# Two decoder layers with gated cross attention and expert routing: roots, slots and weighted bias rows move from VectorE to GpSimd, and the turning of exponentials stands one quarter row further behind the scores

## The reference

```python
# 32 batches, 128 query rows, 120 context rows, width 128, 16 heads of 8, 8 experts, top 2
x = x + tanh(g_xattn[0]) * xattn0(layernorm(x), ctx, ctx, group_prob, mask)   # softmax * group_prob
x = x + tanh(g_ffn[0])   * ffn0(layernorm(x))        # top-2 of 8 experts with a capacity, gelu, 512 hidden
x = x + tanh(g_xattn[1]) * xattn1(layernorm(x), ctx, ctx, mask1)
x = x + tanh(g_ffn[1])   * ffn1(layernorm(x))        # all 8 experts, weighted by the top-2 scores

def layernorm(x, eps=1e-5):
    m, v = mean(x, -1), var(x, -1)
    return (x - m) / sqrt(v + eps)
# ffn0: probs = softmax(x @ Wg); the top two with gates; position of a token in its expert by a running
# count; tokens past the capacity are dropped; rows scattered to the experts, gathered back, times gate.
# ffn1: out = sum_e ((h_a * sigmoid(h_b)) @ Wo.T + bo) * comb[e];  h = x @ W1[e].T + b1[e]
```

## Time and profile before

| | |
|---|---|
| median of 3 runs | 1053.52 us (1051.51 to 1056.82) |
| profiled execution, device time | 1046.87 us |
| its span, first to last instruction | 1045.1 us |
| mean granted TensorE clock | 0.902 |
| busy: PE / DVE / ACT / POOL | 76% / 64% / 59% / 54% |

### The profile page before, as it was taken

One profiled execution on the slowest core, in us unless ns is written; L12 is line 12 of the kernel. 1 busy time (PEld: TensorE's weight loads), 2 busy tenths in 40 slices (PEclk: granted clock), 3 DMA queues, 4 the chain that ended last, 5 costly groups with the idle time before them and its releaser, 6 DMA issues.

```text
span 1045.1 us, 20666 instructions
## 1 busy us (share of the span) xinstructions
PE 796.5 (76%) x6552; PEld 627.2 (60%) x6552; DVE 668.9 (64%) x1992; ACT 611.4 (59%) x2578; POOL 559.8 (54%) x762
## 2 busy tenths in 40 slices
PE   2379888878852899990156778677877799999997
PEld 1256665656641799990035555555655577888885
DVE  1369989889863222210347778789888878666664
ACT  1369888778840444440146877687888645444442
POOL 7355566686556000002676875865421176777775
PEclk9679999999985899996558998999999899999998
DMA  7869734565334222225136365633530000000000
GB/s 179 207 175 272 163 94 112 110 157 131 89 86 164 62 72 71 72 59 161 45 81 146 99 146 98 151 96 59 124 72 12 21 21 21 21 21 21 11 11 21
DMA packets 80069, 97.56 MB, mean 93 GB/s; under 512 B 7952, under 2 KB 67285, under 8 KB 79000
## 3 DMA queue, kind: packets, MB, share of 16 engines
q1 hardware_dynamic: 75864, 87.99, 33.0%
q0 software_dynamic: 4096, 8.25, 3.3%
HBM read 59.18 MB, written 41.58 MB: 96 GB/s over the span
## 4 chain that ended last, share of the span: by engine, by line
PE 27%; issue 26%; POOL 18%; DVE 16%; ACT 10%; DMA 2%; POOLq 0%; SPq 0%; DVEq 0%; ACTq 0%
ACT exp L640 7%; PE psum L557 5%; PE psum L559 5%; PE psum L558 5%; POOL got_rows L1214 4%; DVE shift L815 4%; POOL scratch_xe L1207 3%; PE psum L407 3%; POOL full L1175 2%; PE psum L420 2%; PE psum L383 1%; DVE exp_T L825 1%; POOL ln_rstd L1143 1%; POOL parts L1185 1%; DVE ln_stats L785 1%
## 5 line engine op out<-in xcount | busy, mean ns | idle before, releaser
L640 ACT ACTIVATE exp<-psum,shift 128x120 f32<-128x120 f32 x1024 | 362.8, 400 | 140.4 <-DVE shift L815 139.6
L640 ACT ACTIVATION_READ_ACCUMULATOR exp<-psum,shift 128x1 f32 x1024 | 246.3, 244 | 0.0
L407 PE MATMUL psum<-ident,exp 128*120 128x128 f32 x1024 | 169.5, 291 | 79.5 <-ACT exp L640 47.5
L815 DVE TENSOR_REDUCE shift<-psum 128x4 f32<-128x480 f32 x256 | 165.5, 646 | 64.2 <-PE psum L398 63.6
L407 PEld LDWEIGHTS psum<-ident,exp 128*120 128x120 f32 x1024 | 118.6, 144 | 114.9 <-ACT exp L640 112.2
L1279 POOL TENSOR_TENSOR q_operand<-q_operand 128x512 f32<-128x512 f32 x96 | 126.1, 1313 | 61.8 <-DVE q_operand L1088 57.0
L1088 DVE SCALAR_TENSOR_TENSOR q_operand<-psum,comb,q_operand 128x256 f32<-128x256 f32 x256 | 111.5, 478 | 66.4 <-ACT q_operand L753 66.3
L753 ACT ACTIVATE q_operand<-psum 128x512 f32<-128x512 f32 x128 | 76.3, 599 | 112.9 <-PE psum L559 112.8
L395 PE MATMUL psum<-neg_rows,const_bf 128*128 128x480 bf16 x256 | 98.7, 385 | 35.8 <-issue 19.7
L557 PE MATMUL psum<-w_T_high,xn_T_high 128*128 128x512 f32 x256 | 106.9, 417 | 5.4 <-DVE w_T_low L1054 4.2
L559 PE MATMUL psum<-w_T_high,xn_T_low 128*128 128x512 f32 x256 | 101.3, 396 | 0.0
(11 more groups left out here) (135 smaller groups left out, 1649.9 us busy)
## 6 DMA issues: line engine op xcount, KB each, us to landing
q_operand<-scratch_q SPq DMA_DIRECT2D x32, 384.0 KB, 6.3
k_operand<-scratch_k SPq DMA_DIRECT2D x32, 360.0 KB, 9.3
scratch_q<-parts SPq DMA_DIRECT2D x16, 384.0 KB
scratch_k<-parts SPq DMA_DIRECT2D x16, 360.0 KB
scratch_q<-parts SPq DMA_DIRECT2D x16, 256.0 KB
scratch_xe<-in_zero_rows SPq DMA_DIRECT2D x8, 512.0 KB, 11.2
scratch_k<-parts SPq DMA_DIRECT2D x16, 240.0 KB
xe_rows<-scratch_xe SPq DMA_DIRECT2D x16, 192.0 KB, 2.7
```

The source lines that it names most:

```text
L407: ins = pe.transpose(ps[0:S2, T_BANKS[G % 2], u * S:(u + 1) * S], atts[l].expS[:, G % RING_E, u, :], ident[:, :])
L640: ins = act.activation(atts[l].expS[:, G % RING_E, u, :], ps[:, S_BANKS[G % 3], u * S2:(u + 1) * S2], ACT.Exp, bias=atts[l].shift[:, i % 2 ...
L815: dve.tensor_reduce(atts[l].shift[:, i % 2, 4 * r:4 * r + 4], ps[:, S_BANKS[G % 3], 0:4 * S2].rearrange("p (h k) -> p h k", h=4), AX_X, AL ...
```

## The change

- `rstd` leaves VectorE. Its Newton step is done in `powers` on GpSimd, as four dependent instructions on 128x4 values; the product with the mean is dropped, as normalising now subtracts the mean and multiplies by the root. Normalising of the far tables moves from offset 6 to 5.
- `slots` moves to GpSimd, as nine instructions (the integer slot is written by a copy of its own), in `POST` offset 24; sends wait for count 23 of `rt`.
- `add_bo` moves to GpSimd: one product over four batches into a new buffer `bo_part`, one addition. The sum of the weights stays on VectorE, at the end of `combination`.
- The lags of turning, inverse, inverse rows, sums and scaling each grow by one slot, and with them all `POST` steps. The ring of exponential buffers has four instead of three entries.
- ScalarE's `take_exps` of layer 1 stands before the exponentials of its slot instead of behind them.

```diff
@@ -49,7 +49,7 @@
 RING_O = 8
-RING_E = 3
+RING_E = 4
@@ -60,9 +60,9 @@
-LAG_TURN, LAG_INV, LAG_ROWS, LAG_SUM, LAG_O = 2, 5, 7, 8, 9
...
-ROUTE_STEPS = 25
+LAG_TURN, LAG_INV, LAG_ROWS, LAG_SUM, LAG_O = 3, 6, 8, 9, 10
...
+ROUTE_STEPS = 26
 WEIGH_STEPS = 17
@@ -89,10 +89,10 @@
 NEAR = dict(k_project=0, k_take=1, k_part0=1, k_left0=1, k_part1=2, k_left1=2, k_out=(1, 2, 3), k_fetch=12,
-            stat=0, power=1, rstd=2, norm=3, turn=4, turned=5, bias=8,
+            stat=0, power=1, norm=3, turn=4, turned=5, bias=8,
             q_project=5, q_take=6, q_part0=6, q_left0=6, q_part1=7, q_left1=7, q_out=(6, 7, 8), q_fetch=12)
 FAR = dict(k_project=0, k_take=1, k_part0=2, k_left0=3, k_part1=3, k_left1=4, k_out=(5, 7, 9), k_fetch=16,
-           stat=0, power=2, rstd=4, norm=6, turn=10, turned=11, bias=10,
+           stat=0, power=2, norm=5, turn=10, turned=11, bias=10,
            q_project=14, q_take=15, q_part0=16, q_left0=17, q_part1=17, q_left1=18, q_out=(19, 21, 23), q_fetch=26)
@@ -101,7 +101,7 @@
-POST = dict(stat=0, power=2, rstd=4, norm=6, turn=10, turned=11, gate=14, logits=15, top=16, one_hot=17, exp=18,
+POST = dict(stat=0, power=2, norm=5, turn=10, turned=11, gate=14, logits=15, top=16, one_hot=17, exp=18,
             ranks=21, take_ranks=22, positions=23, slots=24, send=26, weigh=22, add_bo=23)
@@ -242,6 +242,7 @@
     csum = sb(feed, "comb_sum", [S, 4, CB])
+    bo_part = sb(feed, "bo_part", [S, CB, D])
     with ExitStack() as mem:
@@ -277,7 +278,7 @@
     e_w, e_up, e_gelu, e_down, e_y, y_out = sem("e_w"), sem("e_up"), sem("e_gelu"), sem("e_down"), sem("e_y"), sems("y_out", 3)
-    gather, combine, ld_bo1, vbo_done = sems("gather", RING_Y), sem("combine"), sem("ld_bo1"), sem("f_bo")
+    gather, combine, ld_bo1, vbo_done, bo_part_done = sems("gather", RING_Y), sem("combine"), sem("ld_bo1"), sem("f_bo"), sem("bo_part")
     c_exp, f_xT, xT_out, xT_in, ld_last, f_less, ld_b1 = sem("c_exp"), sem("f_xT"), sem("xT_out"), sems("xT_in", 2), sems("ld_last", 2), sem("f_less"), sem("ld_b1")
@@ -697,10 +698,10 @@
                 early(l, s)
+                if l == 1 and r == (LAG_TURN + 3) % 4 and 0 <= s - LAG_TURN < 4 * B:
+                    take_exps(l, *divmod(s - LAG_TURN, 4))
                 if i < B:
                     exps(l, i, r)
-                if l == 1 and r == (LAG_TURN + 3) % 4 and 0 <= s - LAG_TURN < 4 * B:
-                    take_exps(l, *divmod(s - LAG_TURN, 4))
                 behind(l, s)
@@ -784,21 +785,9 @@
             on.wait_ge(ln_stats[who], CB * (n + 1))
-            on.wait_ge(ln_rstd[who], 4 * n)
+            on.wait_ge(ln_norm[who], CB * n)
             for b in range(CB):
...
-        def rstd(who, n):
-            r_s, m_v = rs[:, who], mv[:, who]
-            y, t_, r, m_r = (r_s[:, j, :] for j in range(4))
-            on.wait_ge(ln_pow[who], 2 * n + 2)
-            dve.tensor_tensor(t_, y, y, ALU.mult).then_inc(ln_rstd[who], 1)
-            on.wait_ge(ln_rstd[who], 4 * n + 1)
-            dve.scalar_tensor_tensor(t_, r_s[:, 4, :], -0.5, t_, ALU.mult, ALU.mult).then_inc(ln_rstd[who], 1)
-            on.wait_ge(ln_rstd[who], 4 * n + 2)
-            dve.scalar_tensor_tensor(r, t_, 1.5, y, ALU.add, ALU.mult).then_inc(ln_rstd[who], 1)
-            on.wait_ge(ln_rstd[who], 4 * n + 3)
-            dve.scalar_tensor_tensor(m_r, m_v[:, :, 0], -1.0, r, ALU.mult, ALU.mult).then_inc(ln_rstd[who], 1)
@@ -893,23 +882,6 @@
-        def slots(n):
-            sl = slice(n * CB, (n + 1) * CB)
-            on.wait_ge(rt, step_count(n, 15))
-            dve.tensor_scalar(slot_get[:, :, sl], dest[:], float(SLOTS - 1), None, ALU.min).then_inc(rt, 1)
-            dve.tensor_scalar(tmp[:], keep[:], -SKIP, SKIP, ALU.mult, ALU.add).then_inc(rt, 1)
-            on.wait_ge(rt, step_count(n, 16))
-            dve.tensor_copy(run_b[:], run_f[:]).then_inc(rt, 1)
-            on.wait_ge(rt, step_count(n, 17))
-            dve.tensor_tensor(gate_e[:, 1, :], gate_e[:, 1, :], gate_e[:, 0, :], ALU.mult).then_inc(rt, 1)
-            on.wait_ge(rt, step_count(n, 19))
-            dve.tensor_tensor(slot_put[:, :, sl], dest[:], tmp[:], ALU.add).then_inc(rt, 1)
-            on.wait_ge(rt, step_count(n, 22))
-            dve.tensor_scalar(tmp[:], keep[:], tg_f[:, 0:1], None, ALU.mult).then_inc(rt, 1)
-            on.wait_ge(rt, step_count(n, 23))
-            for j in range(TOPK):
-                dve.tensor_tensor(slot_w[:, j, sl], gate_e[:, j, :], tmp[:, j, :], ALU.mult).then_inc(rt, 1)
@@ -934,17 +906,8 @@
-        def add_bo(c):
-            n = NCH + c
             on.wait_ge(rt, step_count(n, 15))
             dve.tensor_reduce(csum[:, 0, :], comb[:, c], AX_X, ALU.add).then_inc(rt, 1)
-            on.wait_ge(rt, step_count(n, 16))
-            on.wait_ge(ln_norm[1], CB * (n + 1))
-            on.wait_ge(vbo_done, 1)
-            for b in range(CB):
-                ins = dve.scalar_tensor_tensor(x[:, c * CB + b, :], vbo[:], csum[:, 0, b:b + 1], x[:, c * CB + b, :], ALU.mult, ALU.add)
-            ins.then_inc(rt, 1)
@@ -972,14 +935,10 @@
                     stat_rows(0, C, l, P)
-                if o == at["rstd"]:
-                    rstd(0, C)
             for j in range(NCH):
...
                     stat_rows(1, n, l, j)
-                if o == POST["rstd"]:
-                    rstd(1, n)
                 if o == POST["top"]:
@@ -991,13 +950,9 @@
                         positions(n)
-                    if o == POST["slots"]:
-                        slots(n)
                 else:
...
                         combination(j)
-                    if o == POST["add_bo"]:
-                        add_bo(j)
@@ -1098,7 +1053,6 @@
         stat_rows(0, 0, 0, 0)
-        rstd(0, 0)
         on.wait_ge(tanh_done, 2)
@@ -1115,7 +1069,6 @@
         stat_rows(0, NCH, 1, 0)
-        rstd(0, NCH)
         for i in range(CB, 2 * CB):
@@ -1141,6 +1094,15 @@
             pool.tensor_tensor(r_s[:, 0, :], r_s[:, 4, :], half_c[:, :], ALU.pow).then_inc(ln_pow[who], 1)
+            y, t_, r = (r_s[:, j, :] for j in range(3))
+            on.wait_ge(ln_pow[who], 2 * n + 2)
+            pool.tensor_tensor(t_, y, y, ALU.mult).then_inc(ln_rstd[who], 1)
+            on.wait_ge(ln_rstd[who], 4 * n + 1)
+            pool.tensor_tensor(t_, r_s[:, 4, :], t_, ALU.mult).then_inc(ln_rstd[who], 1)
+            on.wait_ge(ln_rstd[who], 4 * n + 2)
+            pool.tensor_scalar(t_, t_, -0.5, 1.5, ALU.mult, ALU.add).then_inc(ln_rstd[who], 1)
+            on.wait_ge(ln_rstd[who], 4 * n + 3)
+            pool.tensor_tensor(r, t_, y, ALU.mult).then_inc(ln_rstd[who], 1)
@@ -1153,7 +1115,7 @@
             for b in range(CB):
-                pool.tensor_scalar(xn[:, slot, b, :], x[:, c * CB + b, :], r_s[:, 2, b:b + 1], r_s[:, 3, b:b + 1], ALU.mult, ALU.add).then_inc(ln_norm[who], 1)
+                pool.tensor_scalar(xn[:, slot, b, :], x[:, c * CB + b, :], mv[:, who, b, 0:1], r_s[:, 2, b:b + 1], ALU.subtract, ALU.mult).then_inc(ln_norm[who], 1)
@@ -1200,12 +1162,40 @@
+        def slots(n):
+            sl = slice(n * CB, (n + 1) * CB)
+            on.wait_ge(rt, step_count(n, 17))
+            pool.tensor_scalar(slot_get[:, :, sl], dest[:], float(SLOTS - 1), None, ALU.min).then_inc(rt, 1)
+            pool.tensor_scalar(tmp[:], keep[:], -SKIP, SKIP, ALU.mult, ALU.add).then_inc(rt, 1)
+            pool.tensor_copy(run_b[:], run_f[:]).then_inc(rt, 1)
+            pool.tensor_tensor(gate_e[:, 1, :], gate_e[:, 1, :], gate_e[:, 0, :], ALU.mult).then_inc(rt, 1)
+            on.wait_ge(rt, step_count(n, 19))
+            pool.tensor_tensor(tmp[:], dest[:], tmp[:], ALU.add).then_inc(rt, 1)
+            on.wait_ge(rt, step_count(n, 22))
+            pool.tensor_copy(slot_put[:, :, sl], tmp[:]).then_inc(rt, 1)
+            on.wait_ge(rt, step_count(n, 23))
+            pool.tensor_scalar(tmp[:], keep[:], tg_f[:, 0:1], None, ALU.mult).then_inc(rt, 1)
+            on.wait_ge(rt, step_count(n, 24))
+            for j in range(TOPK):
+                pool.tensor_tensor(slot_w[:, j, sl], gate_e[:, j, :], tmp[:, j, :], ALU.mult).then_inc(rt, 1)
...
             b, j = divmod(m, TOPK)
-            on.wait_ge(rt, step_count(c, 22))
+            on.wait_ge(rt, step_count(c, 23))
             on.wait_ge(zeroed, 16 * -(-SLOTS // 1024))
...
+        def add_bo(c):
+            n = NCH + c
+            on.wait_ge(rt, step_count(n, 16))
+            on.wait_ge(ln_norm[1], CB * (n + 1))
+            on.wait_ge(vbo_done, 1)
+            xs = x[:, c * CB:(c + 1) * CB, :]
+            pool.tensor_tensor(bo_part[:], vbo[:].rearrange("p (o d) -> p o d", o=1).broadcast_to([S, CB, D]),
+                               csum[:, 0, :].rearrange("p (b o) -> p b o", o=1).broadcast_to([S, CB, D]), ALU.mult).then_inc(bo_part_done, 1)
+            on.wait_ge(bo_part_done, c + 1)
+            pool.tensor_tensor(xs, xs, bo_part[:], ALU.add).then_inc(rt, 1)
@@ -1251,6 +1241,10 @@
                     normalise_rows(1, l * NCH + j, j)
+                if l == 0 and o == POST["slots"]:
```

(3 more changed lines are left out.)

## The result

The changed kernel takes 1081.2 us (median of 4 runs, 1079.92 to 1081.89) beside 1053.35 us for the kernel before: ratio 1.026, 95% interval 1.023 to 1.029. It is 28 us slower. The forecast was 1031 and faster, so the sign was wrong.

A forecast was written before the change was run, and what follows sets the result against it. It took waits in a loop among engines, not one engine, to bound full attention chunks; layer gains less start and tail costs summed to -21.5 us, span 1023.6, forecast 1031 against the 1053.52 median, range 1012 to 1049.

The forecast's parts named there:

- What bounds the kernel: Attention stages: no engine saturated; full chunks lose 4 to 7 us to a loop of waits among engines.
- (d): Turning a slot later, four exponential buffers: PE interruptions free up to about 2.7 us instead of about 1.3.
- (e): ScalarE's outlet ahead of its exponentials in layer 1: PE's 30.3 us of waits should nearly vanish.
- (a) to (c): Moves from VectorE to GpSimd: root 1.3 us each, slots 2.6 us and bias rows 2.6 us of GpSimd time.
- (f): GpSimd's queue from spread of v to spread inverse: 17.3 us, 14.6 after cover; layer 0 full chunk 32.0 instead of 34.1.
- normalising 1.8: Item in GpSimd's layer 0 list between spread of v and spread inverse: normalising takes 1.8 us of 17.3.
- GpSimd's own floor: GpSimd per full layer 0 chunk: busy 24.35, gaps about 2, new work 5.2, giving 31.6 us.
- the cover of 2.7 us: PE's stand of some 5 us for the spread inverse: 2.7 us hidden by three score groups ahead of ScalarE.
- Rival 1: GpSimd's v-to-inverse block, uncovered, takes over in full chunks: +12 us, 1065; chance 0.08.
- Rival 2: GpSimd's whole cycle, not its block, sets full chunks, halving the gain: -7 us, 1046; chance 0.2.
- The mark set beforehand: Sign that the forecast is wrong: PE's waits for the spread inverse exceed 60 us, from 21.9 before.
- Layers: Attention stages: layer 0 full chunks -6 and neighbours -5; layer 1 full chunks -10.5 and lighter stretches -5.5 us.

The follow-up runs named there:

- outlet_behind: lag_alone with ScalarE's outlet put behind its exponentials again: 1037.16 us, 0.986 of the kernel before.
- form_alone: Kernel before with only normalising's form changed to subtract and multiply, root still on VectorE: 1067.93 us, 1.018.
- norm_form: Changed kernel with normalising multiplying and adding again, mean product as two more small GpSimd instructions: 1060.96 us, 1.012.
- early_power: Kernel before plus lags, outlet in front and bias rows on GpSimd; statistics at -1, power 0, VectorE's root 2: 1026.27 us, 0.977.
- early_root: Kernel before plus lags, bias rows and roots on GpSimd, slots on VectorE; multiply-and-add normalising at 6, statistics -1, power 0: 1020.29 us, 0.973.
- lag_alone: Kernel before with only the later lags, fourth exponential buffer and ScalarE's outlet in front; roots, slots, bias rows on VectorE: 1023.26 us, 0.977.
- root_early: Changed kernel with far statistics at offset -1 and power with root at 0, ahead of the spread of v: 1063.84 us, 1.013.
- norm_six: Changed kernel with the far normalising back at offset 6, behind the spread inverse: 1070.79 us, 1.018.

## Why the prediction was wrong

- **What bounds the kernel, and (d), (e)**: right in kind, small in size. I gave lags and outlet no sum of their own; alone they gain 2.3%, 24.6 us, more than the whole forecast of 21.5 (a sum that on 1053.52 gives 1032, not 1031). For (e), whose 30.3 us of waits did go, `outlet_behind` shows 14 us of time, 9.6 of them in the stage it touches.
- **(a) to (c), prices**: right. Root 1.13 us (1.3 forecast), slots 2.2 to 2.4 (2.6), bias rows 2.3 (2.6); the tail +7.3 us (+5).
- **(f), the step that failed.** Its list says "normalising 1.8": four times the 0.461 of before, though the diff changes the two operations and where one operand comes from. It is 3.15. An edit was left unpriced because it looked like bookkeeping of (a), and no row of before showed the new form; it should have had bounds. `form_alone` gives 1.8% for it alone, `norm_form` 1.4% within the change. It counts twice a chunk, so it also breaks the line on GpSimd's own floor, from which the 32.0 was taken: not 31.6 us but 34.1 (a cycle of 38.0 less 3.9 of waits). Two normalisings at 1.35 us over the forecast make about this difference. The rest of the block was laid out well: 17.3 forecast, 18.7 measured, 1.35 of the difference this term. Normalising's move from offset 6 to 5, ahead of the spread inverse, I counted into the block but never set against leaving it at 6: 0.8%.
- **(f), the cover of 2.7 us**: PE's interruption was covered for 2.0 us. I took it from the ring of three score groups as if it were full when PE stops; one group was left. Nor did I count that PE restarts at half clock. From one late turning of the inverse to the next (201.17 to 239.16) the chunk took 38.0 us for 32.0: 18.8 up to PE's restart, forecast at 14.6, and 19.2 for the other nine slots, forecast at 16.5, with 6.9 us at 0.55 of the clock and the second slow normalising in them.
- **Rival 1** came true, with 8% and 1065; its threshold (v-to-inverse work over PE's seven slots by more than 2.7 us with nothing regained) was passed, by 18.7 against 14.9. That the missed terms carried it on from 1065 to 1081 fits the 1.4% of `norm_form`. Rival 2's mechanism, GpSimd's cycle, acts beside it in layer 0. The mark set beforehand, waits for the spread inverse over 60 us, showed at 88.2.
- **Layers**: layer 0's attention was forecast at -11 and came at +12.1, layer 1's at -16 and came at +7.3. In layer 1 the same block with five gathers in it stalls PE 7.6 to 9.2 us.
- **Sum of the parts**, from the ratios, each uncertain by about 0.5%, and taken on top of the lags (beside the moves these brought nothing): lags -2.3%, slots +0.95, bias rows -0.25, roots as written +4.5: +2.9, measured +2.6. Of the roots' 4.5, form and place are 2.6, the root's instructions 1.9.
- **Open**: why `early_power` loses in layer 0 what `early_root` gains there; by which wait the form costs 1.8% where it stands behind the spread inverse; and what the half clock costs. The mean granted clock was 0.884 to 0.896 in the runs of the changed kernel and 0.912 to 0.923 in those of `lag_alone`, but no run changes it by itself.

## What to carry over

When an engine off the critical path hands over one thing per cycle that all others wait for, lay out its queue between taking and giving and price every instruction in it, also those whose operands only change form. Then add up its whole cycle too: independent work pays when it is moved to where the engine itself waits (`root_early`), and hardly when it only changes sides of the hand-over (`norm_six`). Count as cover for a stall only the work whose inputs the stalled engine has handed over by then, not the size of the ring between them. And time the halves of a compound change apart: here the reordering gained 2.3% and the moves buried it.
